# Routed tokens of a Macaron block: fewer scatters ahead of the routing list, and gathers of queue 2 held to gate steps

## The reference, cut to what matters

```python
x = x + 0.5 * moe(layernorm(x))          # phase 1 of the routed experts: "e1"
x = x + attention(layernorm(x))          # delta rule, multiscale conv, gated fusion
x = x + 0.5 * moe(layernorm(x))          # phase 2: "e2"

def moe(x):                              # 4096 tokens of 128 floats, 8 experts
    probs, idx = top_k(softmax(x @ gate_w.T), 2)
    for k in range(2):                   # first choice, then second choice
        pos = place of the token among those that chose expert idx[:, k], in token order
        valid = pos < 640                # capacity
        disp[expert, pos] = x            # 8 queues of 640 rows
        out += weight * (silu(disp @ wi_gate) * (disp @ wi_up)) @ wo, back at the token
```

## Time and profile before

| | us |
|---|---|
| median of 3 runs | 1046.64 (1046.37 to 1047.25) |
| the profiled execution: its own time | 1043.97 |
| the profiled execution: its span, first to last instruction | 1042.2 |
| TensorE busy, share of the span | 886.3 (85%) |
| DVE, ACT, POOL busy | 565.2, 384.7, 502.4 |
| mean granted TensorE clock | 0.91 |
| `route` (to the last of the first three gathers) | 0 to 65 |
| phase 1, queues 0 to 15 | 65 to 286 |
| attention | 286 to 812 |
| phase 2 | 813 to 1042 |

### The profile page before, as it was taken

One profiled execution on the slowest core, in us unless ns is written; L12 is line 12 of the kernel. 1 busy time (PEld: TensorE's weight loads), 2 busy tenths in 40 slices (PEclk: granted clock), 3 DMA queues, 4 the chain that ended last, 5 costly groups with the idle time before them and its releaser, 6 DMA issues.

```text
span 1042.2 us, 28123 instructions
## 1 busy us (share of the span) xinstructions
PE 886.3 (85%) x11844; PEld 769.6 (74%) x11844; DVE 565.2 (54%) x1710; ACT 384.7 (37%) x790; POOL 502.4 (48%) x609
## 2 busy tenths in 40 slices
PE   7357999999688788998799879987877598999996
PEld 6346999999566656876577556865566488999996
DVE  6545556555266816583667424482347355556662
ACT  5213444444124422562337231651045243344441
POOL 2568998355600011851176123833342565545667
PEclk9588999999987988999999888996788899999998
DMA  9732676332130200011003200221021444444544
GB/s 295 119 95 63 221 249 212 117 120 89 48 107 2 46 14 9 22 26 34 8 6 80 68 33 19 61 61 36 33 63 62 138 135 158 133 131 113 114 82 45
DMA packets 82107, 90.32 MB, mean 87 GB/s; under 512 B 10120, under 2 KB 68149, under 8 KB 80958
## 3 DMA queue, kind: packets, MB, share of 16 engines
q1 hardware_dynamic: 66814, 65.33, 21.7%
q0 software_dynamic: 15168, 23.21, 9.5%
HBM read 46.70 MB, written 38.25 MB: 82 GB/s over the span
## 4 chain that ended last, share of the span: by engine, by line
PE 66%; DVE 17%; issue 10%; ACT 3%; DMA 2%; another core or an unknown queue 1%; POOL 1%; SPq 0%; DVEq 0%; ACTq 0%; POOLq 0%
PE e_po L875 13%; PE a_pz L1359 8%; PE a_pz L1424 6%; PE e_pg L887 4%; PE e_pu L889 4%; PE e_pg L889 4%; PE e_pg L888 4%; PE e_pu L888 3%; PE e_pu L887 3%; PE e_pt L859 2%; PE a_pp L1463 2%; PE a_pp L1481 2%; PE a_po L1496 1%; PE a_pp L1566 1%; PE a_pc L1530 1%
## 5 line engine op out<-in xcount | busy, mean ns | idle before, releaser
L989 DVE TENSOR_TENSOR e_hid<-e_sg,e_pu 128x320 f32<-128x320 f32 x256 | 124.9, 488 | 190.3 <-ACT e_sg L930 118.0
L930 ACT ACTIVATE e_sg<-e_pg 128x320 f32<-128x320 f32 x256 | 112.0, 438 | 238.9 <-PE e_pg L889 178.4
L282 POOL DMA_INDIRECT queue<-wide_rows,slot x64 | 66.5, 1039 | 145.0 <-PE a_po L1536 79.4
L887 PE MATMUL e_pg<-e_xlo,e_whi 128*128 128x320 f32 x256 | 97.4, 380 | 17.6 <-issue 14.6
L875 PE MATMUL e_po<-expert,e_hid 128*128 128x128 f32 x640 | 85.6, 277 | 5.6 <-DVE e_rows L965 5.1
L875 PE MATMUL e_po<-e_expert,e_hid 128*128 128x128 f32 x640 | 84.0, 275 | 3.8 <-DVE e_rows L965 2.5
L875 PEld LDWEIGHTS e_po<-expert,e_hid 128*128 128x128 f32 x640 | 81.1, 193 | 6.7 <-DVE e_rows L965 5.9
L875 PEld LDWEIGHTS e_po<-e_expert,e_hid 128*128 128x128 f32 x640 | 79.7, 191 | 4.9 <-DVE e_rows L965 3.0
L1098 POOL TENSOR_TENSOR first_rows<-a_inv,a_nmat 128x31 f32<-128x31 f32 (+15 forms) x93 | 52.2, 561 | 60.1 <-DVE a_nmat L1901 53.1
L889 PE MATMUL e_pu<-e_xhi,e_whi 128*128 128x320 f32 x256 | 80.0, 312 | 0.0
L888 PE MATMUL e_pg<-e_xhi,e_wlo 128*128 128x320 f32 x256 | 79.9, 312 | 0.0
(11 more groups left out here) (376 smaller groups left out, 2194.7 us busy)
## 6 DMA issues: line engine op xcount, KB each, us to landing
expert<-wexp_in SPq DMA_DIRECT2D x14, 512.0 KB
e_expert<-wexp_in SPq DMA_DIRECT2D x14, 512.0 KB
line<-blank SPq DMA_DIRECT2D x3, 1310.0 KB
e_xs<-queue SPq DMA_DIRECT2D x12, 327.5 KB
expert<-wexp_in SPq DMA_DIRECT2D x14, 256.0 KB
e_expert<-wexp_in SPq DMA_DIRECT2D x14, 256.0 KB, 2.9
queue<-blank SPq DMA_DIRECT2D x2, 1310.0 KB, 9.8
rows<-e_rows SPq DMA_DIRECT2D x8, 320.0 KB, 2.8
```

The source lines that it names most:

```text
L282: pool.indirect_dma_start(io.queue, bass.IndirectOffsetOnAxis(ap=k.slot[:, j, 1:2], axis=0), k.xn[:, j, :], None, bounds_check=SLOTS - 1, ...
L887: pe.matmul(out, whi[par][:, i, fs], xlo[par][:, cols], start=True, stop=False)
L930: act.activation(sg[n % 2][:], pg[n % 2][:, 0:HALF], ACT.Silu).then_inc(silued, 1)
L989: dve.tensor_tensor(hid[q % 2][:, f, c * HALF:c * HALF + HALF], sg[n % 2][:], pu[n % 2][:, 0:HALF], ALU.mult).then_inc(hidden, 1)
```

## The change

Three numbers, or tables of them, and one wait. EARLY goes from 22 to 17. `SENT_WITH` spreads the other 15 scatters over queues 2 to 7 as 1, 2, 3, 3, 3, 3, where 10 followed queues 4 to 7 as 2, 2, 3, 3. Queue 2's gathers move from `pick` into the loop, so that each is followed by a step of folding, and the n-th of them waits until DVE has counted n + 1 gate steps of queue 0.

```diff
-EARLY = 22
+EARLY = 17
...
-        SENT_WITH = (0, 0, 0, 0, 2, 2, 3, 3)
+        SENT_WITH = (0, 0, 1, 2, 3, 3, 3, 3)
...
                 folding = raw.folding(pool, k, folded)
-                for q in range(3):
+                for q in range(2):
                     pick(q)
                 sent = EARLY
-                for q in range(3, E):
+                for q in range(2, E):
                     rows_read(pool, q - NX)
                     for n in range(CT):
+                        if q == 2:
+                            pool.wait_ge(hidden, n + 1)
                         pick_rows(pool, table, k, q, rows_of(q), n, n + 1, picked[q % NX])
                         next(folding)
                     for _ in range(SENT_WITH[q]):
```

## The result

The changed kernel takes 1059.51 us (median of 4 runs, 1054.86 to 1060.59) against 1046.95 us for the kernel before, run beside it (1046.37 to 1047.66): 12.56 us more. The forecast was 1059.6, in a range of 1054.8 to 1066.5. It was right.

What follows compares the result with a forecast made beforehand. TensorE was taken to bound phase 1, with POOL nearly full and becoming late at queue 7. Lateness 6.5, wait 1.0, landing 4.5 and clock 1.0 sum to 13.0 us; with 1046.64 that is 1059.6 us, range 1054.8 to 1066.5.

Steps and rivals of the forecast that it cites:

- What bounds: Phase 1: TensorE bounds, POOL nearly full beside it; queue 7's last gather is 7.6 us ahead of its turn.
- Slots: POOL's loop: each gather or scatter plus folding is a slot; 45 instead of 35, queue 7's last gather slot 42.
- The bound that I gave for it: Five fewer scatters ahead of the list: DVE and DMA queues freer, 0 to 1 us earlier; 0 taken.
- Pure lateness: Queue 7's last gather written at 159.6 against TensorE's turn at 153.10: 6.5 us late before moving a byte.
- The wait: Queue 2's gathers waiting for queue 0's gate steps: 0 to 4.6 us, 1.0 taken.
- the 5.6 us of phase 2's pace: Queue 0's gate steps 1 to 8 could take 15.6 us as in phase 2, not 21.2; worth nothing here.
- Landing: Queue 7's last gather, from start of write to TensorE's use: 2.65 to 7.2 us, 4.5 taken.
- The rule that I had weighed against the row: Queue 7's gather would not stand behind the clear, sum 2 us smaller; a measured 7.2 us scatter landing spoke against it.
- rival of a fast landing: Queue 7's last gather lands in 2.65 us, same mechanism: 11.2 us more, 1057.8 us; chance 0.20.
- The clock: TensorE's slower clock after its stall at queue 7: 0 to 1.6 us, 1.0 taken.
- Queue 8: Its load, at 174.3 to 178.8, stays just hidden before the turn at 178.2; rival that it ends last: 1061.2, chance 0.12.
- The sum: Whole delay at the end of phase 1, passed on through attention and phase 2: 13.0 us.

Runs made afterwards that it cites:

- B: Chip of one group of follow-up runs, the one like the result's chip; the kernel before took 1042.9 us there, the change had ratio 1.0132.
- C: Chip of another group of follow-up runs; the kernel before took 978.4 us there and was not itself traced.
- the second trace: The changed kernel, unaltered, run and traced again on another chip beside the kernel before: ratio 1.0132 (1.0074 to 1.019).

## Why the prediction was right, point by point

- **What bounds.** POOL's margin of 7.6 us at queue 7 was the number to look for, and it decided. Shown: taking POOL's work away (folding behind scatters) takes three quarters of the loss away on B, adding it alone makes a loss as large on C.
- **Slots.** 2.08 us forecast, 2.07 measured. Queue 7's last gather: forecast 159.6 without a wait, measured 157.38; 2.0 of the 2.2 us are the loop's earlier start, since the list came earlier. The bound that I gave for it, 0 to 1 us, was too small, but it is not shown that the missing scatters did it: the list came at 57.28 and 59.36 in the change's two traces, at 60.99 and 61.74 in two experiments that also send 17 ahead, and at 61.63 and 61.87 before. Pure lateness is so 157.38 - 153.10 = 4.3 us, for 6.5.
- **The wait.** 1.0 us forecast, 0 measured. The steps were always counted in time: the fifth by 77.6, and POOL came to the gather that waits for it at 81.39. Counted gate steps 1, 4 and 8 of queue 0 of the changed kernel, against the earlier trace rows:

```profile
67.34 0.49 DVE L989 TENSOR_TENSOR e_hid<-e_sg,e_pu 128x320 f32<-128x320 f32 x1 [1.38 <-ACT e_sg L930]
...
74.45 0.49 DVE L989 TENSOR_TENSOR e_hid<-e_sg,e_pu 128x320 f32<-128x320 f32 x1 [3.05 <-remote]
...
80.30 0.49 DVE L989 TENSOR_TENSOR e_hid<-e_sg,e_pu 128x320 f32<-128x320 f32 x1
```

  Step 8 comes 13.0 us after step 1, where it was 21.2: more than the 5.6 us of phase 2's pace came back. Since POOL never waited, the waits did not do it. The gathers stand 2.2 us apart instead of 1.25, with folding between them, and five scatters are gone from ahead of them; which of these shortened the stalls was not taken apart on a chip that has them. Chance is unlikely: from the list to queue 2's turn it was 31.2 and 30.6 us in the two traces of the kernel before, and 25.7 to 26.9 in the four of the change and its variants there. As forecast, these 4 to 6 us bought nothing: TensorE waited for POOL.
- **Landing.** 4.5 us forecast, 4.9 measured, and 7.7 in the second trace. Queue 5's, which I had not priced, took 7.2. SP's issues in the changed kernel tell the difference: a clear (L683) and 512 KB of weights (L811) go out 1.7 and 1.1 us before queue 5's gather (124.63), but 0.8 and 1.5 us behind queue 7's (157.38). The last row, queue 8's load, follows the last scatter by 5.9 us:

```profile
122.96 0.53 SPq L683 DMA_DIRECT2D line<-blank  x1
...
123.53 0.46 SPq L811 DMA_DIRECT2D expert<-wexp_in  x1
...
158.19 0.66 SPq L683 DMA_DIRECT2D line<-blank  x1
...
158.90 0.46 SPq L811 DMA_DIRECT2D expert<-wexp_in  x1
...
168.66 0.37 SPq L805 DMA_DIRECT2D first_rows<-queue  x1
```

  The rule that I had weighed against the row (the Trainium skill, "DMA: Bandwidth & Descriptors", "SWDGE vs HWDGE vs iDMA": an engine goes round its queues in turn) did not keep gathers short that met a clear: they took 7.0 to 8.0 us, and 3.6 to 4.8 where there was none. How the engines share their queues no run here shows. The rival of a fast landing, 2.65 us, fell in the changed kernel; the shortest landing at these turns in any trace was 2.9.
- **The clock.** 1.0 us forecast, 2.8 measured: queue 8's turn follows queue 7's by 14.82 us, not 12.06. This is the term that I got most wrong, by size. The windows behind the stall of queue 7, in the changed kernel, columns as in the earlier trace rows (TensorE starts again at 162.28):

```profile
162.00:164.00 2.00, 1.72 (x8) 1.72 (x9) 0.00 (x0) 0.78 (x2) 1.74 (x3) 0.50 0.96 309
...
166.00:168.00 2.00, 2.00 (x10) 2.00 (x9) 0.27 (x1) 0.25 (x1) 2.00 (x5) 0.50 0.10 33
168.00:170.00 2.00, 2.00 (x16) 2.00 (x16) 1.29 (x3) 0.94 (x3) 1.92 (x4) 0.96 0.12 12
```

  Granted clock 0.50 up to 168, and nearly 1.00 from there: some 5.9 us of work at the lower of the two levels, 1.2 GHz, half of it lost. The upper bound, 1.6 us from the earlier trace rows, took the slow time behind a stall for the same everywhere; there it lasted some 3.3 us after TensorE's start at 84.25 (an estimate from the 0.56 of that window).
- **Queue 8.** It did not end last: its turn has no idle time, as forecast; and one more microsecond went between there and the end of phase 1.
- **The sum** at the end of phase 1 is then 4.28 + 0 + 4.90 + 2.76 + 0.99 = 12.93 for 13.0. That it fits so closely is luck: an early list (2.2) and a wait too many (1.0) stood against a clock (1.8), a tail (1.0) and a landing (0.4) too small. The mechanism is right by itself. What carried the uncertainty was the range, 8.2 to 19.9.
- **What I had not seen:** that the margin of 7.6 us belongs to one kind of chip. On the other TensorE waits 9 us for queue 7's gather with 22 scatters ahead of the list and only the waits added, and taking folding away makes the kernel before 1% faster: POOL bounds it there already. I also had not seen that SP's clear and the gather race each other to the turn.

## What to carry to other kernels

When work moves from ahead of a deadline into a loop, count the slots ahead of each later deadline, with everything that rides on a slot; work on an engine that never shows in the chain of waits (POOL before: 1%) still has a margin, and the margin is what a change spends. Work without a deadline, like the folding, belongs behind the last thing that has one (measured on C: 1% faster). And a margin read from one chip's trace should be taken as a margin on that chip.

## What the runs showed of the hardware that was not expected

- **A stall's second price.** Between the turns of two queues it is 12.05 us undisturbed. With the idle time before the second turn taken off, it was 12.12 us behind idle times of 1.79 and 2.91 us, and 13.6 to 14.9 behind fourteen idle times of 3.54 to 9.33 us before the turns of queues 5, 6 and 7: 1.5 to 2.9 us more, and not the more the longer it stood. Between them the traces do not agree: 2.35 us (queue 6, no folding behind the scatters, B) and 2.75 us (queue 2, the change) were followed by 13.7 each, 1.6 us more.
- **Landing of a gather** of 67 KB: 2.65 us with little else moving; at the turns of queues 5 to 7, 3.6 to 4.8 without a clear, 2.9 to 4.9 with the clear issued 0.8 us or more behind it, 7.0 to 8.0 with the clear issued up to 2.7 us ahead of it.
- **The chip.** The same kernel takes 979 us on some chips and 1043 to 1047 on others, though TensorE's pace in the experts' loop is the same. The stalls of queue 0 and the margin at queue 7 differ with it. No experiment was repeated on both kinds of chip, so what its size, or even its sign, would be on the other kind is open; the change lost on the slower kind, and without its waits on the faster.
